# Decoder, first cross attention: group by group on all engines, with keys and values projected inside the scan

## What is computed

```python
x = x + _L0_attn_ref(_layernorm(x), ...)      # state space scan
x = x + _L0_xattn_ref(_layernorm(x), ctx_512, ctx_512, ...)   # cross attention, one head
x = x + _L0_ffn_ref(_layernorm(x), ...)       # 8 experts, top 2, and a shared one
x = x + _L1_attn_ref(_layernorm(x), ...)
x = x + _L1_xattn_ref(_layernorm(x), ctx_512, ctx_512, ...)
x = x + _L1_ffn_ref(_layernorm(x), ...)
```

```python
h = dA * h + d_t[..., None] * B_t[:, None, :] * u_t[..., None]   # over 128 times, 256 features x 16 states
y_t = jnp.einsum('bdn,bn->bd', h, C_t)
...
q = x_ln @ Wq + bq;  k = ctx @ Wk + bk;  v = ctx @ Wv + bv
out = softmax(q @ k.T) @ v
```

## Time and profile before

| | us |
|---|---|
| median of 3 runs | 1060.34 |
| lowest, highest | 1058.89, 1060.54 |
| the profiled execution, its own time | 1065.21 |
| its span | 1063.4 |
| mean granted TensorE clock, share of full | 0.949 |

### The profile page before, as it was taken

One profiled execution on the slowest core, in us unless ns is written; L12 is line 12 of the kernel. 1 busy time (PEld: TensorE's weight loads), 2 busy tenths in 40 slices (PEclk: granted clock), 3 DMA queues, 4 the chain that ended last, 5 costly groups with the idle time before them and its releaser, 6 DMA issues.

```text
span 1063.4 us, 15174 instructions
## 1 busy us (share of the span) xinstructions
PE 916.8 (86%) x5630; PEld 673.6 (63%) x5630; DVE 810.9 (76%) x1447; ACT 547.0 (51%) x982; POOL 419.5 (39%) x400
## 2 busy tenths in 40 slices
PE   6877778777879999998985776899977999999998
PEld 4222223234769888885554555576655889989997
DVE  6799999997575555573888887679974588778886
ACT  6466565562643222227543222556654477667775
POOL 6499999994210010121964344534411001001110
PEclk9989999999988999999988998689998999999999
DMA  6000000000000000100000001000000000000001
GB/s 183 1 0 1 0 1 1 0 1 0 1 1 15 22 25 15 31 1 1 0 1 1 0 1 40 1 2 2 2 1 1 1 1 23 19 20 21 21 21 41
DMA packets 19860, 13.82 MB, mean 13 GB/s; under 512 B 3067, under 2 KB 18313, under 8 KB 19786
## 3 DMA queue, kind: packets, MB, share of 16 engines
q1 hardware_dynamic: 19786, 12.84, 4.2%
HBM read 11.79 MB, written 1.05 MB: 12 GB/s over the span
## 4 chain that ended last, share of the span: by engine, by line
PE 53%; DVE 17%; ACT 4%; issue 2%; POOL 1%; DVEq 0%; ACTq 0%
PE ps L1298 19%; PE ps L1291 17%; PE ps L1469 3%; DVE small L1175 2%; DVE G L1178 2%; PE ps L1643 2%; PE ps L1585 1%; PE ps L1539 1%; DVE R L1136 1%; DVE stats L787 1%; DVE ps L1141 1%; PE ps L1575 1%; DVE ps L1125 1%; DVE R L1127 1%; PE ps L1502 1%
## 5 line engine op out<-in xcount | busy, mean ns | idle before, releaser
L1298 PE MATMUL ps<-xhl,whl 128*128 128x512 f32 x960 | 250.6, 412 | 11.9 <-DVE xhl L809 5.0
L1298 PEld LDWEIGHTS ps<-xhl,whl 128*128 128x128 f32 x960 | 181.9, 196 | 52.0 <-issue 12.6
L759 ACT ACTIVATE G<-ps,w_exp_bi 128x512 f32<-128x512 f32 x128 | 90.2, 704 | 65.7 <-PE ps L1298 57.7
L1291 PEld LDWEIGHTS ps<-R,G 128*128 128x128 f32 x1024 | 119.0, 192 | 6.4 <-DVE G L1221 4.1
L1291 PE MATMUL ps<-R,G 128*128 128x128 f32 x1024 | 119.7, 275 | 3.1 <-DVE G L1221 3.1
L349 POOL TENSOR_TENSOR R<-G,R 128x1024 f32<-128x1024 f32 x43 | 101.6, 2378 | 16.1 <-ACT R L544 16.1
L620 ACT ACTIVATE G<-ps 128x512 f32<-128x512 f32 x72 | 42.8, 598 | 116.1 <-PE ps L1298 115.3
L902 DVE TENSOR_TENSOR_SCAN R<-ps,R 128x1024 f32<-128x1024 f32 x43 | 97.6, 2278 | 6.5 <-POOL R L358 5.7
L760 ACT ACTIVATE G<-ps,ebs 128x512 f32<-128x512 f32 x144 | 102.2, 710 | 0.0
L981 DVE SCALAR_TENSOR_TENSOR X<-ps,cw,X 128x128 f32<-128x128 f32 x272 | 76.3, 343 | 25.8 <-PE ps L1291 25.6
L1221 DVE SCALAR_TENSOR_TENSOR G<-G 128x1024 f32<-128x1024 f32 x72 | 92.2, 1281 | 2.5
(11 more groups left out here) (260 smaller groups left out, 1735.9 us busy)
## 6 DMA issues: line engine op xcount, KB each, us to landing
ew<-in_w_dram SPq DMA_DIRECT2D x24, 128.0 KB, 2.2
R<-in_exp_wi_dram SPq DMA_DIRECT2D x8, 256.0 KB, 2.6
R<-in_exp_wo_dram SPq DMA_DIRECT2D x8, 256.0 KB, 3.1
X<-in_x_dram SPq DMA_DIRECT2D x4, 256.0 KB, 3.8
out_dram<-X SPq DMA_DIRECT2D x4, 256.0 KB, 2.3
w_ctxT<-in_ctxT_dram SPq DMA_DIRECT2D x1, 487.5 KB
ew<-in_sw_dram SPq DMA_DIRECT2D x3, 128.0 KB, 2.3
w_W_in<-in_W_in_dram SPq DMA_DIRECT2D x1, 256.0 KB, 5.1
```

Source lines behind the costliest of these rows:

```text
L759: sc.activation(G[:, 0, slot, m * GT:(m + 1) * GT], banks[:, m, :], ACT.Exp, bias=exp_bias[m])
L1291: ins = mm(bank(o)[:, 0, b * width:(b + 1) * width], lhs(k, b), rhs(k), start=k == 0, stop=k == ks - 1)
L1298: ins = mm(mix(out) if n == N_WIN1 else out, whl[:, wslot(n), i, m * P:(m + 1) * P], rhs, start=k == 0, stop=k == 2)
```

## The change

- **Keys and values inside the scan.** In eight rounds, the states 3, 6, 9 and 12 of groups 1 and 2 (i = 19, 22, 25, 28 and 35, 38, 41, 44), PE puts one group's keys (then one group's values) into bank 4 where `b_row(i + 3)` stood. ACT copies them out after `c_copy(i - 2)` and ahead of the exponentials of round i + 1. PE does `c_row(i)` and `y_sum(i - 2)`, waits for that copy, and only then does `b_row(i + 3)`. kT and vS move to the buffer G5, which nothing else uses then. The context must have landed before the scan.
- **Last round.** `c_row(63)` goes to bank 4 and no longer waits for product 62. Output projection 0 stands ahead of the last two `y_sum`, and the residual and statistics of group 0 ahead of the last `gate_y`.
- **Attention by group.** PE, ACT and DVE get lists in which the steps of the four groups, and two layer norms, alternate. The copy of the transposed probabilities goes from DVE to ACT. POOL's `ln_scale(1)` stands behind the splitting of two expert weights. The first expert matmuls wait for four residuals at a time rather than for all 16.

No matmul, copy or vector operation is added or dropped; they are moved, and one kind of copy changes its engine.

```diff
+KV_STATE = (3, 6, 9, 12)
...
+        makes_kv = lambda i: i // NS in (1, 2) and i % NS in KV_STATE
+        kv_of = lambda i: NG * (i // NS - 1) + KV_STATE.index(i % NS)
+        c_bank = lambda i: 4 if i == NG * NS - 1 else 5
...
-        kT = G[:, 0, 1, 0:B * LK].rearrange("p (b k) -> p b k", b=B)
-        vS = G[:, 1, 0, :].rearrange("p (b d) -> p b d", b=B)
+        kT = G[:, 5, 0, 0:B * LK].rearrange("p (b k) -> p b k", b=B)
+        vS = G[:, 5, 1, :].rearrange("p (b d) -> p b d", b=B)
...
-            ln_scale(1)
...
             split_e0(1)
+            ln_scale(1)
             ln_scale(2)
...
+            def k0_copy(g):
+                act.wait_ge(S["k_mm"], g + 1)
+                sc.copy(kT[:, gb(g), :], bank(4)[:, 0, 0:GB * LK].rearrange("p (b k) -> p b k", b=GB)).then_inc(S["k_ev"], 1)
+
+            def v0_copy(g):
+                act.wait_ge(S["v_mm"], g + 1)
+                sc.copy(vS[0:LK, gb(g), :], bank(4)[0:LK, 0, :].rearrange("p (b d) -> p b d", b=GB)).then_inc(S["v_ev"], 1)
...
                         b_copy(i + 2)
                     if i >= 2 and on_pool(i - 2):
                         c_copy(i - 2)
+                    if makes_kv(i) and kv_of(i) < NG:
+                        k0_copy(kv_of(i))
+                    elif makes_kv(i):
+                        v0_copy(kv_of(i) - NG)
...
-            act.wait_ge(S["y_gated"], NG)
-            keys_and_values(1, k0_copy, v0_copy)
-            for g in range(NG):
+            def queries(g):
...
+            normalize(1, 0)
+            copy_xnT(1, 0)
+            queries(0)
+            normalize(1, 1)
+            copy_xnT(1, 1)
+            queries(1)
+            exponentials(0)
+            normalize(1, 2)
+            probabilities(0)
+            copy_xnT(1, 2)
+            queries(2)
+            normalize(1, 3)
+            copy_xnT(1, 3)
+            exponentials(1)
+            queries(3)
+            probabilities(1)
+            exponentials(2)
+            normalize(2, 0)
+            probabilities(2)
+            exponentials(3)
+            copy_xnT(2, 0)
+            normalize(2, 1)
+            probabilities(3)
+            copy_xnT(2, 1)
+            normalize(2, 2)
+            normalize(2, 3)
...
-            for g in range(NG):
-                normalize(2, g)
-                if 1 <= g < NG - 1:
-                    copy_xnT(2, g - 1)
...
                                     hst[i % 3].rearrange("p (h n) -> p h n", h=HI),
-                                    bank(5).broadcast_to([P, HI, GT]), ALU.mult).then_inc(S["hc"], 1)
+                                    bank(c_bank(i)).broadcast_to([P, HI, GT]), ALU.mult).then_inc(S["hc"], 1)
                 if n == 1 and g:
                     gate_y(g - 1)
-            gate_y(NG - 1)
...
-            layer_norm(1, add_out("a_out", "a_res"))
-
-            dve.wait_ge(S["omega_sp"], 1)
-            v.tensor_scalar(coef[:, 2, :], coef[:, 1, :], -8.0, None, ALU.mult).then_inc(S["coef_done"], 1)
...
-            for g in range(NG):
+            def second_half(g):
                 add_attended(g)
                 ln_stats(2, g)
...
+            first_half(0)
+            gate_y(NG - 1)
+            ln_norm(1, 0)
+            first_half(1)
+            first_half(2)
+            ln_norm(1, 1)
+            score_max(0)
+            first_half(3)
+            ln_norm(1, 2)
+            ln_norm(1, 3)
+            score_max(1)
+            second_half(0)
+            score_max(2)
+            second_half(1)
+            score_max(3)
+            ln_norm(2, 0)
+            second_half(2)
+            ln_norm(2, 1)
+            ln_lower(2, 0)
+            second_half(3)
+            ln_norm(2, 2)
+            ln_lower(2, 1)
+            ln_norm(2, 3)
+            dve.wait_ge(S["omega_sp"], 1)
+            v.tensor_scalar(coef[:, 2, :], coef[:, 1, :], -8.0, None, ALU.mult).then_inc(S["coef_done"], 1)
...
+            def keys(g, copied):
+                pe.wait_ge(S["b_copied"], copied)
+                mm(bank(4)[:, 0, 0:GB * LK], w["Wk0"][:], w["ctxT"][:, gb(g), :].rearrange("p b k -> p (b k)"),
+                   start=True, stop=True).then_inc(S["k_mm"], 1)
+
+            def values(g, copied):
+                pe.wait_ge(S["b_copied"], copied)
+                for b in range(GB):
+                    ins = mm(bank(4)[0:LK, 0, b * D:(b + 1) * D], w["ctxT"][:, g * GB + b, :], w["Wv0"][:], start=True, stop=True)
+                ins.then_inc(S["v_mm"], 1)
+
             def c_row(i):
-                if i and on_pool(i - 1):
+                if i == NG * NS - 1:
+                    pe.wait_ge(S["b_copied"], NG * NS)
+                elif i and on_pool(i - 1):
                     pe.wait_ge(S["c_copied"], n_pool(i - 1))
                 elif i:
                     pe.wait_ge(S["hc"], n_dve(i - 1))
-                broadcast(5, i % NS + NS, i // NS, "c_bcast")
+                broadcast(c_bank(i), i % NS + NS, i // NS, "c_bcast")
...
+            pe.wait_ge(S["w_ctx"], 16 * 6)
             for i in range(NG * NS):
                 g, n = divmod(i, NS)
-                if i + 3 < NG * NS:
+                if makes_kv(i) and kv_of(i) < NG:
+                    keys(kv_of(i), i + 3)
+                elif makes_kv(i):
+                    values(kv_of(i) - NG, i + 3)
+                elif i + 3 < NG * NS:
                     b_row(i + 3)
                 c_row(i)
...
                 if i >= 2:
                     y_sum(i - 2)
-            y_sum(NG * NS - 2)
-            y_sum(NG * NS - 1)
-            for g in range(NG):
-                pe.wait_ge(S["y_gated"], NG)
+                if makes_kv(i):
+                    if kv_of(i) < NG:
+                        pe.wait_ge(S["k_ev"], kv_of(i) + 1)
+                    else:
+                        pe.wait_ge(S["v_ev"], kv_of(i) - NG + 1)
+                    b_row(i + 3)
+
+            def out_projection(g):
+                pe.wait_ge(S["y_gated"], g + 1)
+                if g < 2:
...
+            out_projection(0)
+            y_sum(NG * NS - 2)
+            y_sum(NG * NS - 1)
+            out_projection(1)
+            transpose_xn(1, 0)
+            out_projection(2)
+            queries(0)
+            out_projection(3)
+            scores(0)
+            transpose_xn(1, 1)
+            queries(1)
+            scores(1)
+            probabilities(0)
+            transpose_xn(1, 2)
+            queries(2)
+            attend(0)
+            scores(2)
+            transpose_xn(1, 3)
+            queries(3)
+            scores(3)
+            probabilities(1)
+            attend(1)
+            probabilities(2)
+            attend(2)
             transpose_xn(2, 0)
+            probabilities(3)
+            attend(3)
             transpose_xn(2, 1)
 
...
-            pe.wait_ge(S["pv_res"], B)
...
                     for m in range(M0):
                         if i:
                             pe.wait_ge(S["silu0"], M0 * (i - 1) + m + 1)
+                        else:
+                            pe.wait_ge(S["pv_res"], GB * (m + 1))
                         up(bank(m)[:, 0, :], N_E0 + e, m, g)
                         if i:
                             pe.wait_ge(S["hid0"], M0 * (i - 1) + m + 1)
+                        else:
+                            pe.wait_ge(S["pv_res"], GB * (M0 + m + 1))
                         up(bank(2 + m)[:, 0, :], N_E0 + e, M0 + m, g).then_inc(S["up_mm"], 1)
```

More of the change, by code:

```diff
@@ L592, in keys_and_values, with exponentials @@
                 v_copy(NG - 1)
-            def k0_copy(g):
-                act.wait_ge(S["k_mm"], g + 1)
-                sc.copy(kT[:, gb(g), :], bank(4 + g)[:, 0, 0:GB * LK].rearrange("p (b k) -> p b k", b=GB)).then_inc(S["k_ev"], 1)
-            def v0_copy(g):
-                act.wait_ge(S["v_mm"], g + 1)
-                sc.copy(vS[0:LK, gb(g), :], bank(4 + g)[0:LK, 0, :].rearrange("p (b d) -> p b d", b=GB)).then_inc(S["v_ev"], 1)
-            act.wait_ge(S["y_gated"], NG)
-            keys_and_values(1, k0_copy, v0_copy)
-            for g in range(NG):
+            def queries(g):
                 act.wait_ge(S["q_mm"], g + 1)
                 sc.activation(qT[:, gcols(g)], bank(4 + g)[:, 0, :], ACT.Identity, bias=w["bq0"][:, 0:1]).then_inc(S["q_ev"], 1)
-            for g in range(NG):
+            def exponentials(g):
                 act.wait_ge(S["sc_max"], g + 1)
@@ L612, in _, with probabilities @@
                                   accum_out=small[:, 2, g * GB + b:g * GB + b + 1]).then_inc(S["sc_exp"], 1)
+            def probabilities(g):
+                act.wait_ge(S["pt_mm"], g + 1)
+                sc.copy(prT[0:LK, gb(g), :], bank(4 + g)[0:LK, 0, :].rearrange("p (b q) -> p b q", b=GB)).then_inc(S["pt_ev"], 1)
+            normalize(1, 0)
[24 more added lines that the diff above has]
+            normalize(2, 3)
             def silu_up(i):
@@ L943, in _, with first_half @@
                                 ALU.max, negate=True).then_inc(S["sc_max"], 1)
```

(40 more changed lines are left out.)

2 lines of the change are left out of this document (1 added, 1 removed).

## The result

| | before | changed |
|---|---|---|
| median of the runs, us | 1059.62 (4 runs, 1058.12 to 1060.54) | 1087.72 (4 runs, 1082.47 to 1088.30) |
| ratio, 95% interval | | 1.0256 (1.0221 to 1.0290) |
| span of the profiled execution | 1063.4 | 1080.8 |
| mean granted TensorE clock | 0.949 | 0.946 |

The change costs 28.1 us; 22.1 had been forecast. The execution whose profile follows was the fastest of its four, 1082.47; its three sisters took 1087.28 to 1088.30 with a mean clock of 0.933 to 0.936. So its rows show the mechanism, and the sum is taken from further profiles of both kernels.

What follows compares the result with a forecast made beforehand. The prediction took the scan to be bound by DVE and the attention by steps waiting for each other. Scan waits +20.8, clock +11.4 and attention -10.1 gave +22.1 us: forecast 1082.4 us, range 1069 to 1095.

Steps and rivals of the forecast that it cites:

- Keys and values in the scan: Scan: eight recurrences wait for exponentials standing behind the key or value copy on ACT, +20.8 us.
- Rival 2: Scan: the copies are hidden and cost nothing, so the kernel gets faster, 1050.2 us; chance 0.05.
- The clock: Scan: PE runs dry behind late recurrences and its clock falls in seven of eight rounds, +11.4 us.
- my row for one, 1.63: Scan: price of one clock fall, from two recurrences 4.94 us apart where 3.31 is usual, 1.63 us.
- The work of a slowed round fills part of the next pause: Scan: the reason given for counting seven clock falls in the eight rounds, not eight.
- Rival 1: Scan: the clock holds because PE does sums in every round, +10.7 us, 1071.0 us; chance 0.18.
- Rival 3: Scan: the clock stays low for longer, up to 27 us in all, 1098 us; chance 0.10.
- The attention: Last gate to first expert matmul: 32.2 us instead of 43.4 by alternating groups; net -10.1 us.
- The 0.8 that the forecast set against it: Behind the attention: the first Silu stands behind four norms on ACT, costing 0.8 us.
- Rival 4: Attention: it gains nothing because thinner PE work drops the clock there, +32 us, 1092 us; chance 0.05.

Runs made afterwards that it cites:

- e12: Changed kernel plus three filler matmuls in PE's pause behind each late recurrence, nothing left out; 1076.3 us against 1061.46 before, ratio 1.0139.
- e3: Changed kernel with key/value copies behind the next round's exponentials on ACT and b_row(i + 3) ahead of the sum on PE; 1054.08 us against 1060.95 before.
- e5: Changed kernel with only the key/value copies moved behind the next round's exponentials on ACT; 1060.67 us against 1060.81 before, ratio 0.9992.
- e8: Changed kernel profiled a second time, no edit; 1088.30 us.
- e11: Changed kernel profiled a third time, no edit; 1088.21 us, a single execution.
- e9: Kernel before the change profiled a second time, no edit; 1061.02 us.
- e10: Kernel before the change profiled a third time, no edit; 1059.12 us, a single execution.
- e1: Changed kernel with last round and attention order as before, keys and values still in the scan; 1099.33 us against 1060.95 before, ratio 1.0346.
- e2: Changed kernel without keys and values in the scan; they stand at the start of the new attention; 1060.85 us against 1060.95 before, ratio 0.9994.
- e4: Changed kernel plus two filler matmuls in PE's pause behind each late recurrence, nothing left out; 1078.18 us against 1060.95 before, ratio 1.0158.

## Why the prediction was right, and where it was short

**Keys and values in the scan, +20.8: right.** With the clock held (`e12`) the eight recurrences are late by 21.0 us, 3.41 for the 3.36 of round 19, 2.30 and 2.31 for 2.28, 3.50 for 3.47, 2.40 for 2.39. `e3` and `e5` show that it hangs on the order of the lists: the copy's place on ACT, and behind it the late `b_row` on PE, which does not show while the copy is in front of it and which the forecast did not price. (The working has the exponentials 0.44 us behind the copy's start and then adds 0.48; the trace has 0.46, 116.06 to 116.52, so nothing hangs on it.) Rival 2, hidden copies, needed just that other order; made in `e3`, it gives the faster kernel.

**The clock, +11.4: the right mechanism, its size too small.** In the first profile there were eight falls, not seven. Taking the 21.0 of `e12` away, each costs 1.72, 1.71, 1.68 and 1.42 in group 1, 1.71, 1.70, 1.57 and 1.28 in group 2, in sum 12.8; my row for one, 1.63, was good, and the last fall of each group, for which I had named no recurrence, puts round 32 or 48 back. The last of the eight lasts 6.8 us (230.7 to 237.5) and still costs only 1.28. In `e8` two of the falls last 6.8 us (2.7 and 1.2 us of lateness) and in `e11` one (2.7), and the term, the sum of what is late less 21.0, is 13.8 and 14.4. I had written a pause of 3.2 us; it is 0.68 and 2.11 with one spreading between. "The work of a slowed round fills part of the next pause", my reason for counting one less, held for no round. Rival 1 (1071.0) is refuted by the falls themselves, and `e12` gives their price: it is 14.8 us slower than the kernel before beside it, the changed kernel 28.1, in spite of 1.8 us that the fillers cost. Rival 3 happened in single rounds only; a slow stretch did not keep itself.

The Trainium skill (TensorE: Matmul & The Clock Gate, "HAM oscillation — how this bites in real kernels") describes a kernel whose PE pauses once in every tile and so pays for a slow start of each next one, and has the gap closed as the remedy. The trace agrees with the pattern (eight falls in eight late rounds) and `e12` with the remedy; the pauses there were long waits for transfers, here 2.11 us.

**The attention, -10.1: right in its steps, taken from a long start.** From the last gate to the first expert matmul I walked 32.2 us, and it is 33.3; from the last recurrence 42.5. The walk had every step at full clock, and the last weighted values ran at half: rows of the changed kernel's PE, weighted values of groups 2 and 3.

```profile
318.45 1.16 PE L1475 MATMUL ps<-G 120*128 120x128 f32 x8 [0.67 <-ACT G L622]
...
324.07 2.07 PE L1475 MATMUL ps<-G 120*128 120x128 f32 x8 [1.56 <-ACT G L622]
```

The base was mis-sized, too: 52.40 held a fall of the clock that the kernel before has not in its other two profiles, 51.13. So the gain up to the first expert matmul is 8.6 and not 9.9, where -10.9 had been forecast. The 0.8 that the forecast set against it, for the first Silu behind four norms on ACT, came as walked. The Silu starts 5.95 us behind the first expert matmul (326.64) and started 5.15 behind it (302.60); before, then changed:

```profile
307.75 1.09 ACT L620 ACTIVATE G<-ps 128x512 f32<-128x512 f32 x2
```

```profile
332.59 1.09 ACT L657 ACTIVATE G<-ps 128x512 f32<-128x512 f32 x2
```

Rival 4, a gain eaten by the clock, did not happen: 0.94 in this stage.

**The sum.** Means of two profiles each (`e8`, `e11` less `e9`, `e10`): recurrences +35.7, attention -8.6, first layer's experts +0.8, second layer +0.3, start -0.4, in all +27.8, and the medians say +28.1. Forecast were +32.2, -10.9 and +0.8 for the Silu, which lies in the first layer's experts. Of the 5.7 us that I was short, 3.5 are in the scan (2.7 of them the clock, 0.5 recurrence 5, which moves between profiles of the kernel before by more than that), 2.3 in the attention (1.3 the base, 1.0 the walk), none at the Silu and 0.3 in the second layer, less 0.4 at the start. The first profile of each kernel is left out here: that of before took 1065.21, above each of its four runs, and that of the changed kernel was the fastest of four. With it, over three profiles each, the recurrences are +35.1, the attention -9.1, the first layer's experts -0.3, the second layer -1.1 and the whole span +24.3. So scan and attention stand either way, and beyond the 0.8 of the Silu no cost of the change in the later stages is shown.

**What it says of the halves.** That moving keys and values pays only with the regrouping was not in my sum: in the attention `e1` loses 1.2 us and `e2` gains 0.8, and both together gain 8.6. That each frees time on PE which only the other can use is my reading of the two timelines; no run shows it by itself.

## What to carry to other kernels

Work put into an engine's idle time costs nothing only if nothing that the bound engine waits for stands behind it in that engine's list: find the slack of the next instruction (1.3 us here), not the idle share (20 us in 51), and put the new work behind it. A late start on the bound engine is then paid a second time where PE is starved by it and its clock falls, so look at what PE does in the hole. And take the base of a sum from more than one profile when the clock falls in the stage.

## What the runs showed of the hardware that I had not expected

- The clock fell in a scan where PE worked in every round: in the 3.40 us ahead of the first fall it had paused for 0.68 and 2.11 us. In the first profile each fall put a recurrence behind it 1.3 to 1.7 us back. Two fillers in that hole stopped six of eight falls, three all of them.
- Removing matmuls can slow PE: without keys and values the attention of `e1` ran its queries at half clock, 5.98 us for 3.60.
- Executions of the same kernel differ by where the falls lie: the 23 runs of the kernel before beside `e1` to `e4` reach from 1056.0 to 1066.0 us around 1060.95, more than the steps between several of these kernels.
